# A two-layer sparse graph kernel: one-neighbour tiles without a softmax, two-slot tiles in one group, query products spread over both layers, gathers in small pieces

## The chip, the cores and the metric

The kernel runs on one core of one Trainium2 chip. The metric is the time of one execution on the device in microseconds (us), the median over repeated runs. A profile is one further execution, recorded by the hardware profiler. The engines are TensorE (PE, with its weight load PEld), VectorE (DVE), ScalarE (ACT) and GpSimd (POOL); each works through its instructions in order. SP only issues DMAs.

## What is computed

Two graph layers over N = 2048 nodes of width 512. The adjacency matrix is sparse (each entry is 1 with a chance of 1/1024, some two neighbours a node).

```python
h = relu(layernorm(x))
# layer 0: attention with 16 heads of 32, W_seq, a1, a2
seq = (h @ W_seq).reshape(N, 16, 32)
scores = leaky_relu(s1[i] + s2[j], 0.2) + (1 - adj) * -65500.0
x = x + elu(softmax(scores) @ seq @ W_out + b_out)
h = relu(layernorm(x))
# layer 1: one head
z = scale * (h @ W_q.T + b_q) @ (h @ W_k.T + b_k).T
z = where(z * adj == 0, -10000.0, z * adj)
x = x + relu(softmax(z) @ (h @ W_v.T + b_v))
```

In layer 0 a node without neighbours attends to all nodes with nearly equal penalties; these are the "lone" rows. In layer 1 a node's query and all keys are folded into one product: u = h @ (W_q.T W_k) + bias, and z is u's dot product with a neighbour's h.

## The kernel before, in words

The nodes are ranked by their number of neighbours and handled in 16 tiles of 128 nodes. `ORDER` gives the order of the tiles, `SLOTS` how many neighbour slots the tile at place t has: 1, 1, 1, 1, 0, 8, 2, 5, 2, 4, 2, 3, 2, 3, 2, 3 for t = 0 to 15. Below, "tile t" is the place in this order. Tiles 0 and 1 hold nodes with exactly one neighbour; tiles 2, 3 and 4 have lone rows too.

Up to about 230 us the program normalises x, multiplies by W_seq, finds the neighbours in adj, ranks the nodes and sums the lone rows' attention head by head. `evacuate(15)` on VectorE ends that part; four matmuls (semaphore `tot_mm`) give the totals that `lone_rows(k)` needs.

**Layer 0** is a loop over k = 0 to 15 (to 17 on VectorE), written out on every engine:

- GpSimd gathers a tile's neighbour rows from DRAM, one indirect DMA a slot (`gather`, semaphore `got[t]`). In its loop over t it computes 1/sqrt(var) with a POW (line 1132), stores x1 (line 1133), gathers as `GATHER[t]` says (line 1121), gathers a late tile of x (line 1138) and stores h1 (line 1141).
- VectorE computes attention weights: `scores(g)` (lines 765 to 769), Exp on ScalarE (line 981), `normalise(g)` (777 to 779). `GROUPS` are tiles that share one softmax: tiles 0 to 3 together, each later one alone. `aggregate(t)` multiplies the rows by the weights (line 793) and adds them (794, 797). In step k VectorE does residual(k - 1) (lines 811 to 818), accumulate(k - 2) (833), norm_bias(k - 1) (825), which waits for the POW, lone_rows(k) for k < 3, normalise for tile k + 2, scores for tile k + 4, aggregate(k + 2).
- TensorE does transposes(k), which waits for aggregate(k), the query product of `U_AT[k]`, transposes_h1(k - 2) and project(k) (line 1214). A query product is u of one tile (`queries`, lines 1233 and 1236). The first waits for `lone_done`, since its PSUM banks hold the totals.
- ScalarE copies between them (lines 997, 1004), forms h1 (1018), the two parts of ELU (1026, 1028), and copies u out (`copy_u`, 989 and 990).

After the loop TensorE does the last query products; between them a matmul with ones sums h over all nodes (line 1260, `h_sum_mm`), which VectorE copies. Two query products follow that sum, and VectorE waits for all sixteen copies before its first layer-1 work (line 941).

**Layer 1**: GpSimd gathers h1 rows (`gather1`, line 1146) and adds each output tile to DRAM (`put`, 1151). VectorE does dot products (893), a softmax for the tiles of each of five `PARTS` and `aggregate1` (930). ScalarE does the Exp of a part (1046, 1047), the rest of the attention sum (`base_of`, 1039), the copies of the transposed tiles (1067) and the outputs (1054). TensorE does `transposes1` (1274) and `products` (1287) with W_v, over six PSUM banks.

## Time and profile before

| | |
|---|---|
| median of 3 runs | 508.01 us (506.52 to 508.14) |
| profiled execution | 511.07 us, span 509.3 us |
| PE busy | 392.0 us (77%) |
| DVE busy | 387.9 us (76%) |
| POOL busy | 277.4 us (54%) |
| ACT busy | 245.2 us (48%) |
| chain of waits | DVE 30%, PE 18%, POOL 12% |

The span is what the engines' records cover; the profiled execution's time holds 1.8 us more. Busy shares are means over stages with different limits, so the rows below are read by stage: layer 0 from about 228 to 386 us, layer 1 from there to 494, then the end. In a row of an engine's time line, the bracket is the idle time before the instruction and what released it; "issue" there means that nothing the profile shows was waited for; a wait for a semaphore whose sender the profile cannot tell is shown so too.

### The profile page before, as it was taken

Reading aid. Unit: us, or ns where it says so; the run is one execution under the profiler, and the core shown is the slowest. Engines: PE = TensorE matmul, PEld = TensorE weight load, DVE = VectorE, ACT = ScalarE, POOL = GpSimd, SP = SyncE. Lnnn points to the kernel's source line nnn. Section 1 sums busy time; section 2 is a strip of 40 time slices with the busy share of each in tenths; the row PEclk is TensorE's granted clock in tenths of the full one; section 3 lists DMA queues with packets and bytes.
Section 4 is the critical chain, followed back from the end, with each engine's and each line's share of the span. In section 5 each row is a group of like instructions: output and inputs, shape, how many; then the busy total and the mean of one; then the engine's idle time right before and its main releaser. Section 6 shows DMA issues by size and latency. Waiting matters only on the chain.

```text
span 509.3 us, 6170 instructions
## 1 busy us (share of the span) xinstructions
PE 392.0 (77%) x2018; PEld 280.7 (55%) x2018; DVE 387.9 (76%) x763; ACT 245.2 (48%) x513; POOL 277.4 (54%) x274
## 2 busy tenths in 40 slices
PE   0199999886368998887649899998998196787950
PEld 0187887664267787785336576655577143343520
DVE  1996699998759999898869899879740579997200
ACT  1424696786189999782223343534441242233310
POOL 1640563124568477785668656853547758862330
PEclk9999999998679999899959899999999589888995
DMA  7955399941000134235444423532225657764450
GB/s 268 413 198 175 147 307 348 352 177 64 6 8 5 19 108 107 85 90 168 129 160 115 138 81 121 175 127 82 81 86 161 204 121 163 174 143 62 57 71 3
DMA packets 24196, 70.04 MB, mean 138 GB/s; under 512 B 6113, under 2 KB 6369, under 8 KB 21985
## 3 DMA queue, kind: packets, MB, share of 16 engines
q0 software_dynamic: 14336, 42.63, 31.0%
q1 hardware_dynamic: 8432, 25.38, 13.9%
q10 hardware_dynamic: 1392, 1.61, 1.0%
q8 instruction: 17, 0.28, 0.2%
q14 instruction: 19, 0.15, 0.1%
HBM read 52.48 MB, written 17.12 MB: 137 GB/s over the span
## 4 chain that ended last, share of the span: by engine, by line
DVE 30%; PE 18%; POOL 12%; issue 8%; ACT 2%; DMA 1%; another core or an unknown queue 0%; DVEq 0%; ACTq 0%
PE psum L1287 4%; PE psum L1196 4%; POOL s_shared L1121 4%; PE psum L1236 3%; DVE w_seq L893 3%; DVE s_shared L723 3%; PE psum L1214 3%; DVE s_shared L716 2%; DVE s_shared L714 2%; POOL s_rs L1132 2%; DVE h_t L930 2%; DVE s_x L730 2%; POOL s_shared L1104 2%; DVE s_shared L930 1%; POOL record_dram L1088 1%
## 5 line engine op out<-in xcount | busy, mean ns | idle before, releaser
L969 ACT ACTIVATE s_shared<-psum,seq_all 128x320 bf16<-128x320 f32 x192 | 81.7, 584 | 6.7 <-PE psum L1196 5.6
L1196 PE MATMUL psum<-s_shared 128*128 128x198 bf16 x768 | 74.2, 256 | 2.3 <-POOL s_shared L1104 2.3
L1196 PEld LDWEIGHTS psum<-s_shared 128*128 128x128 bf16 x768 | 69.8, 99 | 7.5 <-POOL s_shared L1104 3.9
L506 PE MATMUL psum<-w_seq,hT 128*128 128x272 f32 x256 | 61.6, 394 | 1.0 <-ACT u_bias_bc L356 1.0
L1236 PE MATMUL psum<-w_qk,s_early 128*128 128x257 f32 (+1 forms) x256 | 60.7, 391 | 0.0
L1214 PE MATMUL psum<-w_out,hT 128*128 128x512 f32 x128 | 59.2, 607 | 0.0
L506 PEld LDWEIGHTS psum<-w_seq,hT 128*128 128x128 f32 x256 | 47.4, 190 | 10.4 <-issue 1.3
L1236 PEld LDWEIGHTS psum<-w_qk,s_early 128*128 128x128 f32 x256 | 49.1, 197 | 7.3
L1104 POOL TENSOR_TENSOR s_shared<-s_shared 128x1056 f32<-128x1056 f32 x16 | 31.2, 1950 | 21.1 <-DVE s_shared L716 21.1
L1121 POOL DMA_INDIRECT s_shared<-seq_dram,tab x28 | 36.1, 1290 | 10.9 <-issue 8.2
L1018 ACT ACTIVATE h_t<-s_x,s_nm,s_rs 128x512 f32<-128x512 f32 x16 | 13.0, 815 | 54.8 <-DVE s_nm L825 54.8
L1214 PEld LDWEIGHTS psum<-w_out,hT 128*128 128x128 f32 x128 | 25.0, 195 | 24.6 <-issue 24.1
L451 DVE FIND_INDEX8 tab<-near,adj_ring 128x8 uint32<-128x2048 f32 x16 | 36.6, 2285 | 0.0
L448 DVE MAX8 near<-adj_ring 128x8 f32<-128x2048 f32 x16 | 36.5, 2283 | 0.0
L226 POOL TENSOR_TENSOR rstd<-veps,power 128x1 f32<-128x1 f32 x16 | 9.0, 562 | 45.2 <-DVE veps L424 45.0
L1151 POOL DMA_INDIRECT out_dram<-s_lone,tab x12 | 20.2, 1679 | 24.7 <-ACT s_lone L1054 23.5
L1132 POOL TENSOR_TENSOR s_rs<-s_ve,power 128x1 f32<-128x1 f32 x16 | 13.8, 862 | 35.3 <-DVE s_ve L818 35.2
L723 DVE TENSOR_SCALAR s_shared<-psum,neg_s 128x320 bf16<-128x320 f32 x64 | 30.7, 541 | 1.2 <-PE psum L1172 1.2
L1287 PE MATMUL psum<-wv_t,bout_bc 128*128 128x512 f32 x64 | 30.8, 627 | 0.0
L1287 PE MATMUL psum<-wv_t,hT 128*128 128x512 f32 x64 | 30.8, 626 | 0.0
L337 ACT ACTIVATE squares<-adj_ring 128x2048 bf16<-128x2048 f32 x16 | 30.4, 1902 | 0.0
L497 PE MATMUL psum<-ident,h_t 128*128 128x128 f32 x64 | 10.9, 298 | 22.8 <-ACT h_t L330 22.8
(242 smaller groups left out, 792.5 us busy)
## 6 DMA issues: line engine op xcount, KB each, us to landing
adj_ring<-in_adj_dram SPq DMA_DIRECT2D x16, 1024.0 KB, 7.5
seq_dram<-seq_all POOLq DMA_DIRECT2D x16, 264.0 KB, 3.5
x_ring<-in_x_dram SPq DMA_DIRECT2D x16, 256.0 KB, 8.0
w_seq<-in_L_gnn_W_seq_dram ACTq DMA_DIRECT2D x1, 1024.0 KB, 7.7
w_q<-in_L_gnn_W_q_dram SPq DMA_DIRECT2D x1, 1024.0 KB, 18.4
w_k<-in_L_gnn_W_k_dram SPq DMA_DIRECT2D x1, 1024.0 KB, 20.4
w_v<-in_L_gnn_W_v_dram SPq DMA_DIRECT2D x1, 1024.0 KB, 6.6
w_out<-in_L_gnn_W_out_dram SPq DMA_DIRECT2D x1, 1024.0 KB, 10.0
```

The source lines that it names most:

```text
L337: act.activation(squares[:, :], adj_ring[:, t % AR, :], ACT.Square, accum_out=square[:, t:t + 1]).then_inc(adj_squared, 1)
L448: step(dve.max(near[:, t, :], adj_ring[:, b, :]))
L451: dve.max_index(record[:, t, 0:TOP], near[:, t, :], adj_ring[:, b, :]).then_inc(adj_searched, 1)
L506: last = pe.matmul(bank[2 + 2 * (t % 2) + i][:, 0:SX // 2], hT[:, t % 2, c * P:(c + 1) * P], w_seq[:, c, i * (SX // 2):(i + 1) * (SX // 2) ...
L723: last = dve.tensor_scalar(ind[i][:, j, PAD:], bank[6 + i][:, 0:LN], neg_s2[:, j - SIGNS, n:n + 1], 2.0, ALU.is_gt, ALU.mult)
L969: last = act.activation(ind[i][:, j, PAD:], bank[4 + i][:, 0:LN], ACT.Sign, bias=seq_all[:, j, D + n:D + n + 1])
L1104: pool.tensor_tensor(split[i][:, :, 2, :], split[i][:, :, 1, :], top_half(split[i][:, :, 1, :]), ALU.subtract).then_inc(r2_done, 1)
L1121: pool.indirect_dma_start(G(t)[:, s, :], None, seq_dram[:, :], bass.IndirectOffsetOnAxis(tab[:, t, s:s + 1], 0)).then_inc(got[t], 16)
L1196: last = pe.matmul(acc(i)[:, k, 0:3 * W2], ind[i][:, j, k * P:(k + 1) * P], rhs.rearrange("p t w -> p (t w)"), start=(j == 0 and k != 1), ...
L1214: last = pe.matmul(bank[2 + k % 2], hidT[:, c * P:(c + 1) * P], w_out[:, c, :], start=False, stop=(c == C - 1))
L1236: last = pe.matmul(bank[4 + 2 * (t % 2) + i][:, 0:hi - lo], h1T(t)[:, c * P:(c + 1) * P], w_qk[:, c, lo:hi], start=False, stop=(c == C - 1))
L1287: last = pe.matmul(bank[2 + t % 6], aT[t % 2][:, c * P:(c + 1) * P], wv_t[:, c, :], start=False, stop=(c == C - 1))
```

## The change

- Tiles 0 and 1 have no scores, weights or aggregate: TensorE transposes their gathered row. Tiles 2 and 3 take the row times `has`, without weights.
- Tile 5's softmax comes first, alone; the five 2-slot tiles 6, 8, 10, 12, 14 share one; the others are alone. `SCORES_AT` puts `scores` in steps 3, 4, 6, 8, 10, 12, and `normalise` one step later. On ScalarE the Exp of scores moves behind ELU.
- residual waits for the first part of ELU for its first half, for the second part for its second.
- Gathered rows lie at fixed places (`LATE`). Nine gathers come first (tiles 6, 8, 7), then two or three in a step.
- Tile 4 has no query product. `U_AT` has one in steps 3 to 6, 8, 10, 12 and 14, four follow before the sum of h, one behind it; 14 and 15 come within layer 1, for k = 4 and 6 (`U1_AT`). The layer-1 products go over four PSUM banks.
- VectorE's constants are computed for tiles 0 to 11 at first, for the others in the last part.

VectorE in step 3 before, from norm_bias(2) (s_nm) to the first addition for tile 5; s_sc are the scores, s_top their maxima and sums, s_early and s_shared the gathered rows.

```order
L825 SCALAR_TENSOR_TENSOR s_nm<-s_mv,s_rs 128x1
L777 TENSOR_REDUCE s_top<-s_sc 128x16
L778 RECIPROCAL s_top<-s_top 128x16
L779 TENSOR_TENSOR s_sc<-s_sc,s_top 128x128
L765 TENSOR_TENSOR s_sc<-s_shared,tab 128x80
L766 SCALAR_TENSOR_TENSOR s_sc<-s_sc 128x80
L767 TENSOR_TENSOR s_sc<-s_sc,s_pen 128x80
L768 TENSOR_REDUCE s_top<-s_sc 128x16
L769 TENSOR_TENSOR s_sc<-s_sc,s_top 128x80
L793 TENSOR_TENSOR s_early<-s_early,s_sc 128x8x512
L794 TENSOR_TENSOR w_seq<-s_early 128x512
```

And now.

```order
L834 SCALAR_TENSOR_TENSOR s_nm<-s_mv,s_rs 128x1
L786 TENSOR_REDUCE s_top<-s_sc 128x16
L787 RECIPROCAL s_top<-s_top 128x16
L788 TENSOR_TENSOR s_sc<-s_sc,s_top 128x128
L775 TENSOR_TENSOR s_sc<-s_shared,tab 128x32 x5
L777 SCALAR_TENSOR_TENSOR s_sc<-s_sc 128x160
L779 TENSOR_TENSOR s_sc<-s_sc,s_pen 128x160
L780 TENSOR_REDUCE s_top<-s_sc 128x80
L781 TENSOR_TENSOR s_sc<-s_sc,s_top 128x160
L805 TENSOR_TENSOR s_early<-s_early,s_sc 128x8x512
L806 TENSOR_TENSOR w_seq<-s_early 128x512
```

Before, a normalisation is followed by the scores of tile 7 (128x80). Now five additions, one a 2-slot tile, and four operations of 160 elements stand between it and the multiplication for tile 5.

GpSimd from the first gathers of layer 0 on, before: L1121 are gathers (s_shared), L1132 the POW, L1133 the store of x1, L1138 a gather of x, L1141 the store of h1.

```order
L1121 DMA s_shared<-seq_dram,tab 128x528 x7
L1132 TENSOR_TENSOR s_rs<-s_ve,power 128x1
L1133 DMA out_dram<-s_x,tab 2048x512
L1121 DMA s_shared<-seq_dram,tab 128x528 x6
L1141 DMA h_dram<-h_t,tab 2048x512
L1132 TENSOR_TENSOR s_rs<-s_ve,power 128x1
L1133 DMA out_dram<-s_x,tab 2048x512
L1121 DMA s_shared<-seq_dram,tab 128x528 x2
```

And now, up to the third POW and what follows it.

```order
L1132 DMA s_shared<-seq_dram,tab 128x528 x9
L1143 TENSOR_TENSOR s_rs<-s_ve,power 128x1
L1144 DMA out_dram<-s_x,tab 2048x512
L1132 DMA s_shared<-seq_dram,tab 128x528 x2
L1152 DMA h_dram<-h_t,tab 2048x512
L1143 TENSOR_TENSOR s_rs<-s_ve,power 128x1
L1144 DMA out_dram<-s_x,tab 2048x512
L1132 DMA s_shared<-seq_dram,tab 128x528 x2
L1152 DMA h_dram<-h_t,tab 2048x512
L1143 TENSOR_TENSOR s_rs<-s_ve,power 128x1
L1144 DMA out_dram<-s_x,tab 2048x512
L1132 DMA s_shared<-seq_dram,tab 128x528 x2
```

Seven first gathers have become nine, six behind the first POW two; the last two shown, behind the third POW, are tile 14's.

TensorE in layer 1 before, from transposes1(4): L1274 are transposes1, L1285 and L1287 products.

```order
L1274 MATMUL psum<-ident,h_t 128x128 x4
L1285 MATMUL psum<-bias_rows,ones_b 128x512
L1287 MATMUL psum<-wv_t,bout_bc 128x512 x4
L1285 MATMUL psum<-bias_rows,ones_b 128x512
L1287 MATMUL psum<-wv_t,hT 128x512 x4
L1274 MATMUL psum<-ident,h_t 128x128 x4
L1274 MATMUL psum<-ident,s_shared 128x128 x4
```

And now, where L1248 and L1251 are a query product.

```order
L1291 MATMUL psum<-ident,h_t 128x128 x4
L1302 MATMUL psum<-bias_rows,ones_b 128x512
L1304 MATMUL psum<-wv_t,bout_bc 128x512 x4
L1248 MATMUL psum<-bias_rows,ones_b 128x257
L1251 MATMUL psum<-w_qk,s_early 128x257
...
L1302 MATMUL psum<-bias_rows,ones_b 128x512
L1304 MATMUL psum<-wv_t,hT 128x512 x4
L1291 MATMUL psum<-ident,h_t 128x128 x4
L1291 MATMUL psum<-ident,s_shared 128x128 x4
```

Product 14 stands between products(3) and products(4), ahead of transposes1(5). Product 15 stands in the same way behind products(5).

The diff, cut to its core:

```diff
-NSLOT = FIRST_SLOT[T]
+NSLOT = FIRST_SLOT[T] - 4
-GROUPS = [(0, 4)] + [(t, 1) for t in range(FULL, T)]
-GATHER = {0: (8, 9), 1: (10,), 2: (11,), 3: (12,), 6: (13,), 7: (14,), 8: (15,)}
-U_AT = {**{k: (k - 3,) for k in range(3, 12)}, 13: (9,), 15: (10,)}
+GROUPS = [(5,), (6, 8, 10, 12, 14), (7,), (9,), (11,), (13,), (15,)]
+SCORES_AT = {3: 1, 4: 2, 6: 3, 8: 4, 10: 5, 12: 6}
+PLACE = {t: p for p, t in enumerate(t for g in GROUPS for t in g)}
+SCORE = {t: sum(SLOTS[i] for i in PLACE if PLACE[i] < PLACE[t]) for t in PLACE}
+LATE = {6: 0, 8: 2, 10: 4, 12: 6, 14: 8, 7: 10, 9: 15, 11: 10, 13: 15, 15: 0}
+FREED_BY = {11: 7, 13: 9, 15: 8}
+GATHER = {0: ((10, 0, 2),), 1: ((12, 0, 2),), 2: ((14, 0, 2),), 3: ((9, 0, 2),), 4: ((9, 2, 4),), 6: ((11, 0, 3),), 8: ((13, 0, 3),), 10: ((15, 0, 3),)}
+NO_SLOT = 4
+U_SEQ = [t for t in range(T) if t != NO_SLOT]
+U_NO = {t: i for i, t in enumerate(U_SEQ)}
+U1_AT = {4: 14, 6: 15}
+U_AT = {3: 0, 4: 1, 5: 2, 6: 3, 8: 5, 10: 6, 12: 7, 14: 8}
...
+            return late[:, LATE[t]:LATE[t] + n, :]
...
+                def group(g):
+                    tiles = GROUPS[g]
+                    K, n, o, p = SLOTS[tiles[0]], len(tiles), SCORE[tiles[0]], PLACE[tiles[0]]
+                    seg = sc[:, o:o + n * K, :].rearrange("p (n k) h -> p n k h", k=K)
+                    best = top[:, p:p + n, :]
+                    return tiles, K, n, seg, best, best.unsqueeze(2).to_broadcast([P, n, K, H])
...
                 def scores(g):
-                    for t in range(t0, t0 + n):
+                    tiles, K, n, seg, best, best_k = group(g)
+                    for i, t in enumerate(tiles):
                         dve.wait_ge(got[t], 16 * K)
-                    step(dve.tensor_tensor(seg, lo[:, :, D:SG].rearrange("p (n k) h -> p n k h", k=K), s1, ALU.add))
+                        last = dve.tensor_tensor(seg[:, i, :, :], G(t)[:, :, D:SG], s1_rank[:, t:t + 1, :].to_broadcast([P, K, H]), ALU.add)
+                        step(last)
                     step(dve.scalar_tensor_tensor(seg, seg, ALPHA, seg, ALU.mult, ALU.max))
...
                 def aggregate(t):
+                    if K == 1:
+                        dve.wait_ge(got[t], 16)
+                        step(dve.tensor_scalar(hb, G(t)[:, 0, 0:D], has[:, t:t + 1], None, ALU.mult))
+                        dve.scalar_tensor_tensor(hb, lone[:, t - LONE0, :], has_not[:, t:t + 1], hb, ALU.mult, ALU.add).then_inc(hid_ready, 1)
+                        return
...
                 def residual(t):
                     b = t % 2
-                    dve.wait_ge(elu_exp, t + 1)
+                    dve.wait_ge(elu_in, t + 1)
...
                     step(dve.scalar_tensor_tensor(x1[:, t, :], bank[2 + b], 0.0, x1[:, t, :], ALU.max, ALU.add))
+                    dve.wait_ge(elu_exp, t + 1)
                     dve.scalar_tensor_tensor(x1[:, t, :], e[b], -1.0, x1[:, t, :], ALU.add, ALU.add).then_inc(x1_ready, 1)
...
                 scores(0)
-                normalise(0)
-                aggregate(0)
                 evacuate(H - 1)
-                aggregate(1)
-                scores(1)
                 dve.wait_ge(tot_mm, 1)
                 dve.wait_ge(fac_exp, 1)
                 lone_rows(0)
                 aggregate(2)
-                starts = {t0: g for g, (t0, n) in enumerate(GROUPS)}
                 for k in range(1, T + 2):
...
-                    if k + 2 in starts:
-                        normalise(starts[k + 2])
-                    if k + 4 in starts and k + 4 > FULL:
-                        scores(starts[k + 4])
+                    if k == 3:
+                        normalise(0)
+                    if k - 1 in SCORES_AT:
+                        normalise(SCORES_AT[k - 1])
+                    if k in SCORES_AT:
+                        scores(SCORES_AT[k])
                     if k + 2 < T:
                         aggregate(k + 2)
...
+                    if t0 == EARLY:
+                        constants(EARLY, T)
...
-                dve.wait_ge(u_copied, T)
+                constants(0, EARLY)
...
-                    if k + 4 in starts and k + 4 > FULL:
-                        exp_scores(starts[k + 4])
...
                         act.activation(e[k % 2], e[k % 2], ACT.Exp, scale=-1.0).then_inc(elu_exp, 1)
-                copy_u(T - 4)
-                copy_u(T - 3)
+                    if k in SCORES_AT:
+                        exp_scores(SCORES_AT[k])
+                copy_u(9)
+                copy_u(10)
+                copy_u(11)
                 copy_h1T(T - 1)
-                copy_u(T - 2)
-                copy_u(T - 1)
+                copy_u(12)
+                copy_u(13)
...
+                    if k in U1_AT:
+                        copy_u(U1_AT[k])
...
-                def gather(t):
-                    if freed_by(t):
-                        pool.wait_ge(hid_ready, freed_by(t))
-                    for s in range(SLOTS[t]):
+                def gather(t, lo, hi):
+                    if t in FREED_BY:
+                        pool.wait_ge(hid_ready, FREED_BY[t] - 1)
+                    for s in range(lo, hi):
...
 
                 pool.wait_ge(mm_done, H)
-                gather(FULL + 1)
-                gather(FULL + 2)
+                for t in (6, 8, 7):
+                    gather(t, 0, SLOTS[t])
...
-                    for k in GATHER.get(t, ()):
-                        gather(k)
-                    if 1 <= t <= T // 2:
+                    for part in GATHER.get(t, ()):
+                        gather(*part)
+                    if 2 <= t < 2 + T // 2:
                         pool.wait_ge(lone_done, LONE)
-                        pool.indirect_dma_start(x1[:, T // 2 + t - 1, :], None, x[:, :],
-                                                bass.IndirectOffsetOnAxis(own[:, T // 2 + t - 1, :], 0)).then_inc(x_late[t - 1], 16)
...
                 def transposes(k):
-                    pe.wait_ge(hid_ready, k + 1)
+                    if k < 2:
+                        pe.wait_ge(got[k], 16)
+                    else:
+                        pe.wait_ge(hid_ready, k - 1)
                     if k:
                         pe.wait_ge(hidT_done, k)
+                    rows = early[:, k, 0:D] if k < 2 else hid[k % 4]
...
                 def queries(t):
-                    pe.wait_ge(h1T_done, t + 1)
-                    if t >= 2:
-                        pe.wait_ge(u_copied, t - 1)
-                    else:
-                        pe.wait_ge(lone_done, LONE)
+                    pe.wait_ge(h1T_done, h1_no(t))
+                    pe.wait_ge(lone_done, LONE)
+                    used = [U_NO[i] for i in U_SEQ if i < t and u_bank(i) == u_bank(t)]
+                    if used:
+                        pe.wait_ge(u_copied, used[-1] + 1)
...
+                pe.wait_ge(evac_done, H - 1)
                 for k in range(T):
                     transposes(k)
-                    for t in U_AT.get(k, ()):
-                        queries(t)
-                    if k >= 2:
+                    if k == 0:
+                        pe.wait_ge(evac_done, H)
...
+                        last.then_inc(tot_mm, 1)
+                    if k in U_AT:
+                        queries(U_AT[k])
+                    if k >= 2 and k - 2 != NO_SLOT:
                         transposes_h1(k - 2)
                     project(k)
-                queries(T - 5)
                 transposes_h1(T - 2)
-                queries(T - 4)
-                queries(T - 3)
+                queries(9)
+                queries(10)
+                queries(11)
                 transposes_h1(T - 1)
+                queries(12)
                 pe.wait_ge(summed, T)
                 pe.wait_ge(hidT_done, T)
                 pe.matmul(bank[0], ones[:, 0:P], h_acc).then_inc(h_sum_mm, 1)
-                queries(T - 2)
-                queries(T - 1)
+                queries(13)
...
                 def products(t):
                     pe.wait_ge(aT_done, t + 1)
-                    if t >= 6:
-                        pe.wait_ge(o_ready, t - 5)
+                    if t >= 4:
+                        pe.wait_ge(o_ready, t - 3)
...
                         transposes1(k)
                         products(k - 1)
+                    if k in U1_AT:
+                        queries(U1_AT[k])
```

## Rows read from the trace of the kernel before

**Rows 1.** Stages: us and length, engines' busy time (instructions), clock, DMA share, GB/s.

```profile
280.00:362.00 82.00, 74.96 (x309) 49.72 (x308) 72.22 (x167) 35.89 (x74) 51.41 (x46) 0.98 0.35 116
```

**Rows 2.** VectorE in time: start, us, line, operation, [idle before <-releaser].

```profile
232.30 0.68 DVE L791 TENSOR_TENSOR w_seq<-s_early,s_sc 128x512 f32<-128x512 f32 x1
...
256.52 0.16 DVE L825 SCALAR_TENSOR_TENSOR s_nm<-s_mv,s_rs 128x1 f32<-128x1 f32 x1 [2.77 <-POOL s_rs L1132]
...
263.64 0.69 DVE L811 SCALAR_TENSOR_TENSOR s_x<-psum,s_x 128x512 f32<-128x512 f32 x1 [1.10 <-ACT bout_bc L1028]
...
282.79 0.18 DVE L777 TENSOR_REDUCE s_top<-s_sc 128x16 f32<-128x32 f32 x1
...
283.51 0.19 DVE L765 TENSOR_TENSOR s_sc<-s_shared,tab 128x32 f32<-128x32 f32 x1
...
284.52 1.22 DVE L793 TENSOR_TENSOR s_shared<-s_shared,s_sc 128x1024 f32<-128x1024 f32 x1
...
354.49 0.68 DVE L811 SCALAR_TENSOR_TENSOR s_x<-psum,s_x 128x512 f32<-128x512 f32 x1
...
362.09 0.68 DVE L811 SCALAR_TENSOR_TENSOR s_x<-psum,s_x 128x512 f32<-128x512 f32 x1
...
395.06 0.28 DVE L941 TENSOR_SCALAR hT<-seq_all 128x16 f32<-128x16 f32 x1 [8.40 <-issue]
```

**Rows 3.** TensorE in time, columns as in rows 2.

```profile
261.18 0.59 PE L1233 MATMUL psum<-bias_rows,ones_b 128*128 128x257 bf16 x2 [9.51 <-DVE s_lone L847]
...
261.56 6.18 PE L1236 MATMUL psum<-w_qk,s_early 128*128 128x257 f32 x16
...
372.88 0.38 PE L1233 MATMUL psum<-bias_rows,ones_b 128*128 128x257 bf16 x2
...
376.57 0.60 PE L1223 MATMUL psum<-ident,h_t 128*128 128x128 f32 x4
...
384.84 1.02 PE L1260 MATMUL psum<-s_shared,ones 128*128 128x512 f32 x2
...
433.88 1.07 PE L1274 MATMUL psum<-ident,s_shared 128*128 128x128 f32 x4 [4.94 <-DVE s_shared L930]
...
439.92 3.60 PE L1287 MATMUL psum<-wv_t,hT 128*128 128x512 f32 x8
...
443.36 0.60 PE L1274 MATMUL psum<-ident,s_shared 128*128 128x128 f32 x4
...
447.83 1.11 PE L1274 MATMUL psum<-ident,h_t 128*128 128x128 f32 x4 [3.88 <-DVE h_t L930]
```

**Rows 4.** The chain of waits: start, us, what.

```profile
455.18 4.20 DMA w_out<-h_dram,tab
```

**Rows 5.** GpSimd in time, columns as in rows 2.

```profile
231.84 0.94 POOL L1121 DMA_INDIRECT s_shared<-seq_dram,tab  x1 [2.61 <-PE psum L1196]
...
239.63 1.15 POOL L1121 DMA_INDIRECT s_shared<-seq_dram,tab  x1 [0.30 <-issue]
...
270.07 4.85 POOL L1121 DMA_INDIRECT s_shared<-seq_dram,tab  x1 [0.30 <-issue]
...
325.26 0.81 POOL L1132 TENSOR_TENSOR s_rs<-s_ve,power 128x1 f32<-128x1 f32 x1
...
326.26 1.05 POOL L1133 DMA_INDIRECT out_dram<-s_x,tab  x1 [0.19 <-issue]
...
327.62 0.98 POOL L1121 DMA_INDIRECT s_shared<-seq_dram,tab  x1 [0.31 <-issue]
...
335.22 0.59 POOL L1132 TENSOR_TENSOR s_rs<-s_ve,power 128x1 f32<-128x1 f32 x1
```

**Rows 6.** The eight gathers of x rows in the loop (line 1138).

```profile
DMA to landing us min/median/max: 3.3/3.7/3.9
```

**Rows 7.** ScalarE in time, columns as in rows 2.

```profile
367.77 0.58 ACT L1004 ACTIVATE hT<-psum 128x512 f32<-128x512 f32 x1
...
446.36 0.22 ACT L1046 ACTIVATE hT<-hT 128x24 f32<-128x24 f32 x1 [1.77 <-DVE hT L910]
```

124 lines of the change are left out of this document (53 added, 71 removed).

## Prediction

> **What bounds the kernel now.** I read the page's stages first, then the two busiest engines in order of time from 228 us on (the diff changes nothing of what runs before that), then the chain of waits. k is a step of the first layer's loop; R(t) is the start of residual(t) on VectorE, which opens step k = t + 1.
>
> From 280 to 362 us VectorE and TensorE are both nearly full: 72.2 and 75.0 us busy in 82 [rows 1]. VectorE hardly ever waits there; a step is its own work plus the short wait for the POW on GpSimd. R(2), R(12) and R(13) stand at 263.64, 354.49 and 362.09 [rows 2]. Two places before are different: norm_bias(1) waits 2.77 us, because GpSimd issues six gathers between two POWs, and residual(2) waits 1.10 us for ScalarE [rows 2]. TensorE stands 9.51 us for lone_done before its first query product [rows 3]. After R(13) TensorE's order decides: the column sum of h ends at about 385.9 [rows 3]. Then VectorE stands 8.40 us, until query tiles 14 and 15 are copied, and begins its first dot product's preparation at 395.06 [rows 2]. In the second layer VectorE, GpSimd (the last gather of h lands 4.20 us after its issue [rows 4]) and, over the last 27 us, TensorE follow each other.
>
> **The change part by part**, as shifts of times against the profiled execution (minus is earlier).
>
> *Up to R(2).* Tiles 0 and 1 lose their softmax and their product, but VectorE then only waits longer for the totals from TensorE, since evacuate(15), which ends where the product of 232.30 starts, comes no sooner: nothing. Tile 2 loses a product of 0.7 as that one [rows 2], but seven first gathers become nine. They begin at 231.84 and the seventh ends at 240.78 [rows 5], 1.28 each, so the ninth ends near 243.4 and POW(0) after it: norm_bias(0) gains 0.3 only. Tile 3 loses its product: 0.7. With two gathers instead of six behind POW(0), the wait of 2.77 falls to about 0.7: 2.0. Tile 6's own scores leave: 1.0, the length 283.51 to 284.52 of another 2-slot tile [rows 2]. ScalarE's Exp of scores now stands behind the ELU and no longer holds it: 1.1. Sum -5.1. Waiting for elu_in alone before the first half of residual adds nothing where VectorE is late anyway.
>
> *Steps 3 to 13.* Five 2-slot softmaxes become one. Left out: five normalisations of 0.72 (282.79 to 283.51) and four more scorings of 1.01 [rows 2], -7.6. Added: five first additions of 0.22 and four wide operations of about 0.4, 2.7; one wide normalisation, 1.5. The wide ones, of 160 elements, are estimates from the 0.2 that an operation of 32 takes, five of them in 1.01 [rows 2]. The scores of tiles 7, 9, 11, 13 and 15 only move.
>
> Then a **new wait**. scores(1), of all five tiles, stands in step 3 directly behind normalise(0) and ahead of aggregate(5), and it needs tile 14's two rows. Their gathers are issued in the same step, behind POW(2) and the store of x1. From the end of a POW: 0.19 and 1.05 for the store, 0.30, 0.98 for a gather, 0.31; the second gather starts 2.8 us after the POW [rows 5]. Landing takes 3.3 to 3.9 us in the eight gathers of x rows [rows 6], so 6.5 after the POW. VectorE is there after about 2.0 (normalise(0) and four additions, an estimate from rows 2). It stands 4.5 us, with aggregate(5) and all later steps behind it. Bounds: 0, if the landing were hidden, and 6, with the 4.20 us landing [rows 4] and a held-up issue.
>
> GpSimd is the other new limit. A step in which it issues three gathers, an x row and two stores lasts 9.96 us from POW to POW (325.26 to 335.22) [rows 5]. Before, VectorE's step beside it was about 8.7. Now the gathers of tiles 11, 13 and 15 lie beside steps of 8.9, 7.6 and 7.6 (354.49 to 362.09 is one with three slots and no scores [rows 2]). The third has no x row: 8.7. Waits: 0.8, 2.2 and 1.0, together 4.0, of which 1.1 stood in the old sum. Bounds 0 and 6.
>
> Sum of steps 3 to 13: -7.6 + 2.7 + 1.5 + 4.5 + 4.0 - 1.1 = +4.0. So R(13) shifts by -1.1 only.
>
> A gather is lengthened while VectorE multiplies: the one at 270.07 took 4.85 us beside the multiplication of 4096 elements that began at 269.67, against 0.98 of another [rows 5]. That is in the 9.96. The Trainium skill ("SBUF — State Buffer", Who interferes with whom) infers that a tensor_tensor does not hinder the writing of descriptors, though it contends with a GpSimd operation that reads SBUF. By the first, the three-gather step would be some 1.1 us shorter and the sum 2.5 us lower, near 500.4. The 4.85 us row speaks for the second, as a gather reads its indices; I stay with the row.
>
> *The end of layer 0.* Steps 14 and 15. Before, h's column sum ended 23.8 after R(13). Now project(15) waits for the copy of hidden(15), which ends 6.3 after R(13) (368.35 before [rows 7]) and which a query product used to cover. Then in TensorE's order: project(15) 3.65 (eight matmuls of this size last 3.60), transposes 0.44, three products of 3.69, transposes 0.44, one more 3.69, the sum's matmuls 1.06 [rows 3]: 26.7 after R(13), +2.9. Removing queries from the steps before helps little, since four stand ahead of the sum as before. TensorE has just stood 2 to 3 us. After longer waits its work took longer: a query product 6.18 after 9.51 idle, against 3.69, and 9.5 from 433.88 to 443.36 after 4.94 idle, for transposes and two products that take 7.7 at full clock [rows 3]. I add half of the smaller loss, 0.8; bounds 0 and 4.2, both losses.
>
> *Between the layers.* constants(0, 12) needs only copies that were made long before. The 8.40 us go: -8.4, with product 13 beside VectorE's dots. The gathers of h then lead the first dot by 8 instead of 12 us. Dot 3's row is issued fourth and lands about 7.5 us after the first issue: in time.
>
> *Layer 1.* Product 14 (3.69) falls before TensorE's 4.94 us wait, and is hidden. Product 15 falls before the 3.88 us wait [rows 3]; but ScalarE's Exp at 446.36 [rows 7] stands behind the transposes that it delays. These move from 443.36 to 445.4 only, since with the shorter wait ahead the 1.8 us lost to the clock come back, and their copy is done near 446.6. I count 0.3. Four PSUM banks instead of six for the outputs cost nothing: each output was read more than a product earlier. The second constants call adds two small operations, 0.45. Sum +0.75; bounds 0 and 7.8.
>
> Total: -5.1 + 4.0 + 3.7 - 8.4 + 0.75 = -5.1. The profiled execution took 511.07 us (span 509.3, 1.8 around it) and becomes 506.0. The median of the runs shown is 3.1 below it, and I take the shift from there: 508.0 - 5.1 = 502.9.
>
> **Rivals.** *The gathers are in time.* The waits for tile 14 and behind three gathers do not come: -4.5 and -4.0, 494.4. For it: GpSimd is often idle before a POW in the old trace. Against: the four intervals worked out above all come from its rows.
>
> *Layer 1 pays for the products.* TensorE runs in order, and the transposes behind each product feed ScalarE, whose Exp feeds VectorE, whose weights release the output, the store ahead of the last gathers, and so the last dots. If the waits at 433.88 and 447.83 cover nothing, two products come in full, 7.4 instead of 0.3: 510.0, slower. It turns the sign once 5.4 of the 7.4 stay on the path (the 5.1 gained and the 0.3 counted already). Against: both covers stand in the rows, 8.8 us in all.
>
> *Every late gather waits twice.* Tiles 11, 13 and 15 are gathered two steps ahead of their aggregation, no longer three. If each row lands 1.7 us after VectorE asks for it, on top of the POW, 5.1 come back: 508.0, and the change does not do what it says, splitting work without shortening the path.
>
> **How the numbers follow.** Forecast 0.52 (499.5 to 506), gathers in time 0.18, layer 1 pays 0.16, late gathers wait twice 0.14. Below 495.5 lies over half of the second case, above 509 over half of the third: 2 in 10 are outside. What a measurement of this kernel can tell from no change is about 0.3%, 1.5 us. Faster: 0.51 + 0.18 + 0.03 = 0.72. Same: 0.01 + 0.02 + 0.07 = 0.10. Slower: 0.14 + 0.04 = 0.18.
>
> **What would show it.** VectorE standing 4 to 5 us within step 3, released by a gather and followed by the 4.4 us multiplication. R(13) within 2 us of 362. POWs about 10 us apart where three gathers stand, with norm_bias waiting 1 to 2.7. The sum's matmuls 25 to 29 us after R(13). No wait over 1 us between the copy of that sum and the first dot. Query products 14 and 15 where TensorE stood idle. I am wrong if R(13) comes before 358, or if the second layer lasts over 3 us longer from its first preparation to the end.

## The result and the profile after

| | before | changed |
|---|---|---|
| median of 8 runs | 507.69 us (505.93 to 508.43) | 503.97 us (502.04 to 505.86) |
| ratio | | 0.993, 95% interval 0.9905 to 0.9955 |
| profiled execution, span | 511.07, 509.3 us | 502.33, 500.7 us |
| DVE, PE, POOL busy | 387.9, 392.0, 277.4 us | 379.3, 390.5, 275.3 us |
| chain of waits | DVE 30%, PE 18%, POOL 12% | DVE 27%, POOL 22%, PE 10% |

The time fell by 3.7 us; 5.1 was forecast. The two spans differ by 8.6 us, more than the medians, so the kernel before was profiled a second time (below).

VectorE's time line of the changed kernel: start, length, engine, line, operation, and in brackets the wait before it.

```profile
251.93 0.16 DVE L834 SCALAR_TENSOR_TENSOR s_nm<-s_mv,s_rs 128x1 f32<-128x1 f32 x1 [0.47 <-POOL s_rs L1143]
...
268.01 0.19 DVE L775 TENSOR_TENSOR s_sc<-s_shared,tab 128x32 f32<-128x32 f32 x1 [5.60 <-DMA s_shared<-seq_dram,tab]
...
269.56 4.42 DVE L805 TENSOR_TENSOR s_early<-s_early,s_sc 128x4096 f32<-128x4096 f32 x1
...
308.85 2.29 DVE L805 TENSOR_TENSOR s_shared<-s_shared,s_sc 128x2048 f32<-128x2048 f32 x1
...
317.91 0.16 DVE L834 SCALAR_TENSOR_TENSOR s_nm<-s_mv,s_rs 128x1 f32<-128x1 f32 x1 [1.51 <-POOL s_rs L1143]
...
325.41 1.76 DVE L805 TENSOR_TENSOR s_shared<-s_shared,s_sc 128x1536 f32<-128x1536 f32 x1
...
334.45 0.16 DVE L834 SCALAR_TENSOR_TENSOR s_nm<-s_mv,s_rs 128x1 f32<-128x1 f32 x1 [2.75 <-POOL s_rs L1143]
...
349.74 0.16 DVE L834 SCALAR_TENSOR_TENSOR s_nm<-s_mv,s_rs 128x1 f32<-128x1 f32 x1 [1.50 <-POOL s_rs L1143]
350.43 0.21 DVE L775 TENSOR_TENSOR s_sc<-s_shared,tab 128x48 f32<-128x48 f32 x1 [0.53 <-DMA s_shared<-seq_dram,tab]
...
360.98 0.68 DVE L819 SCALAR_TENSOR_TENSOR s_x<-psum,s_x 128x512 f32<-128x512 f32 x1
...
387.74 0.69 DVE L952 COPY w_seq<-psum 128x512 f32<-128x512 f32 x1 [10.43 <-PE psum L1278]
388.35 0.16 DVE L904 TENSOR_SCALAR hT<-seq_all 128x12 f32<-128x12 f32 x1
...
450.80 0.69 DVE L899 CUSTOM_DVE_ANT_0 w_seq<-seq_all,w_out 128x512 f32<-128x512 f32 x1 [1.63 <-DMA w_out<-h_dram,tab]
```

The reader is to see: the wait of 2.77 for the POW before norm_bias(1) [rows 2] is 0.47; a new wait of 5.60 us stands where the forecast put 4.5, released by a gather and followed by the 4.42 us multiplication for tile 5; three longer waits for the POW stand behind the steps with three gathers; R(13) is at 360.98, 1.1 earlier than in [rows 2], though 0.9 of this lies ahead of E (below), where both kernels do the same; and the 8.40 us between the copy of the column sum and the first preparation of layer 1 are gone (387.74, then 388.35).

GpSimd's time line of the same execution:

```profile
241.20 0.95 POOL L1132 DMA_INDIRECT s_shared<-seq_dram,tab  x1 [0.30 <-issue]
242.17 0.60 POOL L1143 TENSOR_TENSOR s_rs<-s_ve,power 128x1 f32<-128x1 f32 x1
...
309.43 2.56 POOL L1132 DMA_INDIRECT s_shared<-seq_dram,tab  x1 [0.31 <-issue]
...
323.57 0.96 POOL L1143 TENSOR_TENSOR s_rs<-s_ve,power 128x1 f32<-128x1 f32 x1 [1.13 <-DVE s_ve L827]
...
326.06 1.96 POOL L1132 DMA_INDIRECT s_shared<-seq_dram,tab  x1 [0.31 <-issue]
...
333.84 0.58 POOL L1143 TENSOR_TENSOR s_rs<-s_ve,power 128x1 f32<-128x1 f32 x1
...
380.52 0.97 POOL L1157 DMA_INDIRECT s_shared<-h_dram,tab  x1 [2.51 <-DMA h_dram<-h_t,tab]
...
407.05 1.64 POOL L1162 DMA_INDIRECT out_dram<-s_lone,tab  x1 [0.30 <-issue]
...
446.58 0.95 POOL L1157 DMA_INDIRECT w_out<-h_dram,tab  x1 [0.30 <-issue]
```

POW(8) to POW(9) takes 10.27 us with three gathers, where [rows 5] showed 9.96. And from the first gather of h at 380.52 to the last at 446.58 GpSimd has no gap but its usual 0.3. Its share of the chain of waits is 22%, against 12% in the first trace of before and 18% in the second: the chain now runs through these gathers and puts. TensorE's late products stand where it would have waited:

```profile
415.89 3.63 PE L1251 MATMUL psum<-w_qk,s_early 128*128 128x257 f32 x16
...
424.27 0.66 PE L1291 MATMUL psum<-ident,s_shared 128*128 128x128 f32 x4 [0.66 <-DVE s_shared L943]
...
428.64 3.63 PE L1251 MATMUL psum<-w_qk,s_early 128*128 128x257 f32 x16
...
438.62 0.66 PE L1291 MATMUL psum<-ident,h_t 128*128 128x128 f32 x4 [2.26 <-DVE h_t L943]
```

The waits of 4.94 and 3.88 [rows 3] are 0.66 and 2.26, and both products take the 3.63 us of full clock. The transposes and the two products behind the first wait took 9.5 us before and take 7.8 now, 4.15 ahead of product 15 and 3.65 behind it:

```profile
424.98 3.60 PE L1304 MATMUL psum<-wv_t,bout_bc 128*128 128x512 f32 x8
...
439.40 5.22 PE L1304 MATMUL psum<-wv_t,bout_bc 128*128 128x512 f32 x8
```

Behind the 2.26 us that are left of the second wait, eight matmuls still take 5.22 us (second row) and not 3.60.

### The profile page after: what moved, and what is told of

The parts are those of the page before. It is cut to its first block, busy times and chain, and to the rows that moved or that the text cites. A ratio compares the mean times of both kernels' runs of the same rounds, so it can differ in the third digit from the quotient of the medians.

```text
span 500.7 us, 6093 instructions
## 1 busy us (share of the span) xinstructions
PE 390.5 (78%) x1996; PEld 276.8 (55%) x1996; DVE 379.3 (76%) x725; ACT 242.9 (49%) x505; POOL 275.3 (55%) x274
## 4 chain that ended last, share of the span: by engine, by line
DVE 27%; POOL 22%; PE 10%; issue 8%; DMA 3%; ACT 2%; DVEq 0%; ACTq 0%; POOLq 0%
POOL s_shared L1132 4%; PE psum L1304 4%; POOL s_shared L1157 4%; POOL s_x L1157 3%; DVE s_shared L730 3%; PE psum L1207 3%; DVE s_shared L723 3%; DVE s_shared L721 3%; POOL out_dram L1162 3%; POOL s_rs L1143 2%; DVE s_shared L805 2%; DMA s_shared<-seq_dram,tab 2%; POOL s_shared L1115 2%; DVE s_st L823 2%; DVE s_x L821 2%
## 5 line engine op out<-in xcount | busy, mean ns | idle before, releaser
L1229 PE MATMUL psum<-w_out,hT 128*128 128x512 f32 x128 | 61.4, 625 | 0.0
L1251 PE MATMUL psum<-w_qk,s_early 128*128 128x257 f32 x240 | 57.8, 395 | 0.0
L515 PEld LDWEIGHTS psum<-w_seq,hT 128*128 128x128 f32 x256 | 47.4, 190 | 10.4 <-issue 1.3
L1251 PEld LDWEIGHTS psum<-w_qk,s_early 128*128 128x128 f32 x240 | 46.8, 200 | 7.1
L1132 POOL DMA_INDIRECT s_shared<-seq_dram,tab x28 | 34.8, 1243 | 10.9 <-issue 8.2
```

What stands on the lines that cost most here:

```text
L515: last = pe.matmul(bank[2 + 2 * (t % 2) + i][:, 0:SX // 2], hT[:, t % 2, c * P:(c + 1) * P], w_seq[:, c, i * (SX // 2):(i + 1) * (SX // 2) ...
L1132: pool.indirect_dma_start(G(t)[:, s, :], None, seq_dram[:, :], bass.IndirectOffsetOnAxis(tab[:, t, s:s + 1], 0)).then_inc(got[t], 16)
L1229: last = pe.matmul(bank[2 + k % 2], hidT[:, c * P:(c + 1) * P], w_out[:, c, :], start=False, stop=(c == C - 1))
L1251: last = pe.matmul(bank[u_bank(t) + i][:, 0:hi - lo], h1T(t)[:, c * P:(c + 1) * P], w_qk[:, c, lo:hi], start=False, stop=(c == C - 1))
```

## The experiments

The twelve runs were made in three sets, the first on one chip, the others on another; the result above was taken apart from them. All times below are counted from E, the start of evacuate(15)'s last reduction (line 730 before, 737 after), since everything ahead of it is the same work and shifts by up to 2.2 us between executions:

```profile
231.60 0.78 DVE L730 TENSOR_REDUCE s_x<-psum 128x198 f32<-128x594 f32 x1 [0.95 <-PE psum L1196]
...
230.68 0.78 DVE L737 TENSOR_REDUCE s_x<-psum 128x198 f32<-128x594 f32 x1 [2.67 <-PE psum L1207]
```

The first row is of the kernel before, the second of the changed kernel. S is the first preparation of layer 1 on VectorE. "g first" and "g last" are the starts of the first and last gather of h on GpSimd. Each number is the difference of two starts in the run's time lines, or of the span and E.

```
kernel              set  R(2)   R(13)   h sum copied  g first  g last  end     ratio to before
before (rows)        -   32.04  130.49  154.37        151.48   223.58  277.70
changed, first       -   26.14  130.30  157.06        149.84   215.90  270.02  0.993
a0 changed           1   26.13  129.54  156.30        149.79   228.21  282.68  1.001  (0.9982 to 1.0038)
e1 early gathers     1   26.10  124.72  152.16        144.94   223.52  277.52  0.9876 (0.9834 to 0.9919)
e2 spread gathers    1   26.15  127.02  153.78        146.55   226.37  280.72  0.9944 (0.9917 to 0.997)
e4 no group          1   26.15  125.25  152.01        144.79   224.42  279.56  0.9918 (0.9891 to 0.9945)
x1 before            2   32.03  130.60  156.08        153.18   221.34  275.50
x3 late copy         2   26.13  130.01  156.77        149.55   215.78  270.37  0.9941 (0.9919 to 0.9963)
e3 split products    2   26.14  128.36  155.70        148.48   214.68  269.58  0.9914 (0.9885 to 0.9943)
e5 products back     2   26.14  129.73  156.49        149.26   226.67  280.86  1.0136 (1.0116 to 1.0156)
a1 changed           3   26.13  130.18  156.93        149.70   215.71  270.00  0.9956 (0.9935 to 0.9976)
e7 product 9 back    3   26.14  129.69  154.55        151.01   218.24  273.23  0.998  (0.9964 to 0.9996)
e9 put later         3   26.13  129.97  156.73        149.50   213.88  269.63  0.9899 (0.9864 to 0.9934)
e8 all               3   26.10  120.19  146.95        139.71   205.62  259.57  0.9755 (0.9722 to 0.9788)
```

Medians of the kernel before in the three sets: 515.53, 506.83 and 506.57 us.

**Both kernels again.**

> The kernel before once more, for a second trace. In the second trace of the changed kernel TensorE's completion of query product 13 reached ScalarE 8.9 us after its modelled end, and the transposes behind it 5 us after theirs, while GpSimd issued its 21 gathers of h without a gap: those 14 us are the whole loss against the first trace (512.6 against 500.7 us). If such a stall belongs to the gathers' burst, the kernel before has it too where its last products end inside the burst: S (the first preparation of layer 1) or the first Exp of layer 1 would come up to 14 us later than the 395.06 and 399.73 of its first trace, on a machine where its time is near 515; where its time is near 508 it would have none, or the 1 to 3 us of the first trace. If the stall belongs to the changed code alone, the time of the kernel before near 515 must come from somewhere else in its trace.

> The changed kernel a third time, as the measure for the others of this set. Expected 0.993 of the kernel before where ScalarE does not stand in front of layer 1's first Exp, and 1.001 where it does, as it did in the second trace (8.7 us of VectorE there).

> The changed kernel once more, beside the variants of this set, so that they can be compared with it and not only with the kernel before. Expected: its ratio to the kernel before again near 0.993, its norm_bias waits and its 5.6 us wait for tile 14's row in step 3 as in the first trace. If the two profiled executions differ by 2 us or more in span, then the 8.6 us between the two first traces hold that much of chance.

x1: 507.09 us, span 505.3. No stall stands in it. Its first gather of h on GpSimd:

```profile
382.98 0.97 POOL L1146 DMA_INDIRECT s_shared<-h_dram,tab  x1 [2.50 <-DMA h_dram<-h_t,tab]
```

and R(13) and S on VectorE:

```profile
360.40 0.69 DVE L811 SCALAR_TENSOR_TENSOR s_x<-psum,s_x 128x512 f32<-128x512 f32 x1
...
393.89 0.17 DVE L941 TENSOR_SCALAR hT<-seq_all 128x16 f32<-128x16 f32 x1 [7.33 <-ACT seq_all L990]
```

From E to the end it is 2.2 us shorter than the first trace of before: 0.6 longer up to S, 2.8 shorter from there (111.41 us to the end of the span, against 114.24). Against this trace the changed kernel is 5.5 us shorter.

a1: 504.40 us, the times from E within 0.2 us of the first trace. Its medians here and in the result lie 2.2 and 3.7 below the kernel before, its traces 5.5 below x1: both profiled executions of the changed kernel are among its fastest (its runs lie between 501.65 and 506.03 in set 3), and what makes the others slower wasn't seen.

a0 is the surprise: on the first set's chip both kernels were near 515, and no gain can be told there (1.001). Up to the first gather of h it is the changed kernel to 0.8 us. Then this stands on VectorE:

```profile
399.88 0.16 DVE L930 TENSOR_TENSOR hT<-hT,s_others 128x4 f32<-128x4 f32 x1 [8.66 <-issue]
```

on ScalarE:

```profile
398.89 0.39 ACT L998 ACTIVATE seq_all<-psum 128x257 f32<-128x257 f32 x1 [12.93 <-remote]
...
408.72 0.60 ACT L1076 ACTIVATE hT<-psum 128x512 f32<-128x512 f32 x1 [6.50 <-remote]
```

and on TensorE:

```profile
386.32 3.63 PE L1251 MATMUL psum<-w_qk,s_early 128*128 128x257 f32 x16
402.62 1.94 PE L1291 MATMUL psum<-ident,h_t 128*128 128x128 f32 x8 [12.66 <-DVE h_t L943]
```

ScalarE's copy of product 13 begins 8.9 us after the modelled end of that product (389.95), the copy of the first transposes 4.2 us after the eight of them end (404.56). Both wait for TensorE ("remote" names no sender). In e1, e2 and e4 the same copy comes 14.6, 15.4 and 12.5 us after the product's end (VectorE's waits there are 14.24, 15.04 and 12.23), in no trace of sets 2 and 3. The late copy of product 13 lies inside GpSimd's 21 gathers of h without a gap (379.71 to 405.78 in a0); the second late copy comes 2.9 us after them, and sets 2 and 3 have the same 21 gathers and no late copy, so the gathers alone don't make it. Why it happens on one chip and not on the other is open, and whether the kernel before has it there too: it was not profiled on it. So the missing gain of set 1 isn't explained either. And since these waits differ between the traces of set 1, R(13), which lies ahead of them, tells more than its medians.

**The order of two gathers (e1).**

```
-GATHER = {0: ((10, 0, 2),), 1: ((12, 0, 2),), 2: ((14, 0, 2),), ...
+GATHER = {0: ((14, 0, 2),), 1: ((7, 0, 3),), 2: ((7, 3, 5),), ...
-                for t in (6, 8, 7):
+                for t in (6, 8, 10, 12):
```

> The gathers of tile 14 move from behind POW(2) to behind POW(0); tile 7's five go behind POW(1) and POW(2) instead, and those of tiles 10 and 12 ahead of the first POW. Theory A (the wait in step 3 is on the path, and nothing takes it back later): VectorE no longer stands 5.6 us before tile 14's scores, R(3) to R(13) and the first gather of h all come 5 to 6 us earlier, the time falls by 5.6 to about 498.4. Theory B (TensorE, whose project(4) ends only 4 us before the end of that wait, and GpSimd take over): R(3) comes 5 us earlier but R(13) less than 3, and the time falls by under 3 us.

R(13) came 4.8 us earlier than in a0 and 5.6 earlier than in the changed kernel's first trace; the median is 6.1 below a0's. The wait for tile 14 is gone:

```profile
262.79 1.10 DVE L775 TENSOR_TENSOR s_sc<-s_shared,tab 128x32 f32<-128x32 f32 x5
263.92 0.32 DVE L777 SCALAR_TENSOR_TENSOR s_sc<-s_sc 128x160 f32<-128x160 f32 x1
...
265.24 4.42 DVE L805 TENSOR_TENSOR s_early<-s_early,s_sc 128x4096 f32<-128x4096 f32 x1
```

Theory A, which forecast 5 to 6 us. TensorE had room.

**No group (e4).**

```
-GROUPS = [(5,), (6, 8, 10, 12, 14), (7,), (9,), (11,), (13,), (15,)]
-SCORES_AT = {3: 1, 4: 2, 6: 3, 8: 4, 10: 5, 12: 6}
+GROUPS = [(t,) for t in range(FULL, T)]
+SCORES_AT = {k: k - 2 for k in range(3, 13)}
```

> The two-slot tiles have softmaxes of their own again, one step ahead of their aggregation; everything else is as in the changed kernel, the places of the gathers too. By the terms of the prediction the group saves 7.6 - 2.7 - 1.5 = 3.4 us of VectorE's work and costs the wait for tile 14, which measured 5.6: theory A expects R(13) 2.2 us earlier without the group and the time 2.2 lower, near 501.8. Theory B (small operations are cheaper in the shadow of the waits for the POW than counted, or the wait would have stood for another gather anyway): no difference or slower.

The direction held, the size didn't: R(13) 4.3 us earlier than in a0, the median 5.2 lower. From R(2) to R(13) the waits fall from 14.8 to 5.9 us: tile 14's 4.98 go, and of the three behind three gathers only one is left, 1.51 us, since the work that comes back stands beside the gathers. The work itself, what is left of the stretch without the waits, grows from 88.6 to 93.3 us: 4.7 and not 3.4, mostly because tile 6's scores (1.0) come back in these steps too, which the expectation had left out. Net of both, 4.3. With tile 14's gathers where the change puts them, the group costs more than it saves; with e1's order it is ahead of e4 by 0.5 us at R(13).

**Gathers spread, and multiplications split (e2, e3).**

```
-... 6: ((11, 0, 3),), 8: ((13, 0, 3),), 10: ((15, 0, 3),)}
+... 5: ((11, 0, 1),), 6: ((11, 1, 3),), 7: ((13, 0, 1),), 8: ((13, 1, 3),), 9: ((15, 0, 1),), 10: ((15, 1, 3),)}
```

> The three gathers each of tiles 11, 13 and 15 no longer stand in one step: one goes into the step before, two stay. Theory A (GpSimd's issues bound these steps): the waits of norm_bias at the three places, 1.51, 2.75 and 1.50 us, and the 0.53 for tile 15's row fall from 4.9 us over the usual 0.46 to about 2.2 in all (most of it behind POW(8)), R(13) comes 2.7 us earlier and the time falls by 2.7 to about 501.3. Theory B (the waits only move into the short steps, which have no room for one more gather): R(13) and the time within 1 us of the changed kernel.

R(13) 2.5 us earlier than a0, the median 3.3 lower; one wait of 1.52 is left, behind POW(8), and 0.63 for tile 15's row. Theory A: GpSimd's issues bounded these steps.

```
-                    step(dve.tensor_tensor(rows, rows, w, ALU.mult))
+                    if t in (9, 11, 13):
+                        for s in range(K):
+                            last = dve.tensor_tensor(rows[:, s:s + 1], rows[:, s:s + 1], w[:, s:s + 1], ALU.mult)
+                        step(last)
+                    else:
+                        step(dve.tensor_tensor(rows, rows, w, ALU.mult))
```

> The multiplications of tiles 9, 11 and 13 by their weights (2048, 1536, 1536 elements) are made as one instruction per slot of 512. They run beside the first gather of the three steps with three gathers. Theory A (GpSimd's writing of a gather's descriptors is held until VectorE's running multiplication ends; in the trace such a gather ends 0.85 us after the multiplication in four cases out of four): those gathers fall from 2.56, 1.96 and 1.96 us to under 1.6, the waits of norm_bias behind them by 0.7 to 1 each, VectorE pays 0.1 to 0.3 per tile for the extra instructions, and the time falls by 1 to 1.5. Theory B (a tensor_tensor does not hinder descriptor writing; the gather is long for another reason): the gathers stay at 2 to 2.6 us and the time rises by about 0.5.

GpSimd's time line of e3:

```profile
308.75 0.97 POOL L1137 DMA_INDIRECT s_shared<-seq_dram,tab  x1 [0.30 <-issue]
310.02 1.48 POOL L1137 DMA_INDIRECT s_shared<-seq_dram,tab  x1 [0.30 <-issue]
...
324.54 1.49 POOL L1137 DMA_INDIRECT s_shared<-seq_dram,tab  x1 [0.31 <-issue]
```

and VectorE's beside it:

```profile
308.17 2.50 DVE L807 TENSOR_TENSOR s_shared<-s_shared,s_sc 128x512 f32<-128x512 f32 x4
```

The same work in four instructions takes VectorE 2.50 instead of 2.29 us, and the gather beside it 0.97 instead of 2.56, the next 1.48 instead of 1.13; R(13) came 1.65 to 1.95 us earlier than in x3 and the first trace. Theory A for the gathers. The wait for the POW behind the first of the three steps is back at its usual 0.46, the next fell from 2.75 to 1.50, and the last is back at the usual too; but 1.56 us stand before tile 15's scores instead of 0.62 (x3). In the median 501.68 against x3's 503.34 of the same set; the intervals overlap, and the end of the trace came only 0.8 us earlier than in x3, so the gain in the time is not shown.

**The products before layer 1 again (e5), and the late copy of product 13 (x3).**

```
-U1_AT = {4: 14, 6: 15}
+U1_AT = {}
...
-                    if t0 == EARLY:
-                        constants(EARLY, T)
...
-                constants(0, EARLY)
+                constants(0, T)
...
                 copy_u(13)
+                copy_u(14)
+                copy_u(15)
...
                 queries(13)
+                queries(14)
+                queries(15)
```

> Query products 14 and 15 stand behind product 13 again, ahead of layer 1, and one constants call over all 16 tiles waits for the copies of all. The rest is the changed kernel. The prediction says that this wait was worth 8.4 us and layer 1's two products 0.3: theory A expects VectorE to stand about 8.5 us after its copy of the column sum, and the time 7 to 8 us over the changed kernel. Theory B (GpSimd's gathers of h, issued without a gap from about 380 us, bound layer 1, so that VectorE has room there): the wait comes back as VectorE's, but the time rises by 3 to 6 only.

513.35 us, 9.4 above the changed kernel's first median and 10.0 above x3, which is the changed kernel but for one copy and ran in the same set. VectorE's first work of layer 1:

```profile
400.88 0.17 DVE L904 TENSOR_SCALAR hT<-seq_all 128x16 f32<-128x16 f32 x1 [13.16 <-ACT seq_all L997]
```

The wait is 13.16 and not 8.5, for three products and not two follow the sum, and they share one pair of PSUM banks, so that 14 and 15 each wait 0.84 for the copy before. From E, S is 12.7 us later than in the first trace, the end 10.8: about 1.9 of the delay was hidden. Neither theory's size; theory B's reason holds for 1.9 us only. For the rest the late start of VectorE reaches GpSimd, whose first put stands still for ScalarE's output:

```profile
416.21 1.83 POOL L1162 DMA_INDIRECT out_dram<-s_lone,tab  x1 [10.13 <-ACT s_lone L1063]
```

```
-                copy_u(13)
...
+                    if k == 1:
+                        copy_u(13)
```

> The copy of query product 13 no longer stands on ScalarE ahead of layer 1's first Exp; it is made after the second copy of transposed rows. Everything else is the changed kernel. Where the stall shows (9 to 15 us before the first Exp): theory A (only the signal of product 13, the last work ahead of a wait of TensorE, is late) expects the Exp at its usual 0.7 us after VectorE's weights and the time 9 or more us lower; theory B (TensorE itself stands still) expects the first transposes of layer 1 to end late instead, and a gain under 3 us. Where no stall shows: within 0.5 us of the changed kernel, 0.993 of the kernel before.

There was no stall in its set: 0.9941, as expected. It says nothing on the stall, and so whether only the signal of product 13 is late or TensorE itself stands was not tested.

**What sets the start and the length of layer 1 (e7, e9).**

```
-U_AT = {3: 0, 4: 1, 5: 2, 6: 3, 8: 5, 10: 6, 12: 7, 14: 8}
+U_AT = {3: 0, 4: 1, 5: 2, 6: 3, 8: 5, 10: 6, 12: 7, 14: 8, 15: 9}
...
-                copy_u(9)
...
-                queries(9)
```

> Query product 9 stands in step 15 ahead of project(15), where it covers the copy of hidden(15), as in the kernel before, and no longer behind it. The prediction counted 2.9 us for that missing cover. Theory A (the column sum of h sets the start of layer 1): the sum's matmuls end 1.8 us earlier and the time falls by that. Theory B (GpSimd's gathers of h set it, which begin 8.7 us after R(15)): R(15), and the first gather with it, come 1.7 us later, and the time rises by 1 to 1.7.

VectorE's time line of e7 at R(15) and at the copy of the sum:

```profile
374.17 0.69 DVE L819 SCALAR_TENSOR_TENSOR s_x<-psum,s_x 128x512 f32<-128x512 f32 x1 [3.67 <-ACT u_bias_bc L1032]
...
386.42 0.69 DVE L952 COPY w_seq<-psum 128x512 f32<-128x512 f32 x1 [6.74 <-PE psum L1276]
```

The last gather of h:

```profile
450.11 0.95 POOL L1156 DMA_INDIRECT w_out<-h_dram,tab  x1 [0.30 <-issue]
```

The copy of the sum came 2.4 us earlier than in a1, the first gather of h 1.3 later, the last 2.5 later, and the median rose from 504.40 to 505.76 (the intervals of the ratios overlap; in the traces the end came 3.2 later). Theory B: from the changed kernel on, an earlier sum gains nothing, and later gathers of h cost. Only 1.3 of the last gather's 2.5 us come from the start; the other 1.2 are longer issues (the 39 gathers took 41.5 us instead of 40.0), for a reason no trace shows.

```
-                for t in range(9):
+                for t in range(10):
                     gather1(t)
                 for t in range(T):
                     put(t)
-                    if 9 + t < T:
-                        gather1(9 + t)
+                    if 10 + t < T:
+                        gather1(10 + t)
```

> GpSimd issues tile 9's four gathers of h ahead of the first put, so that each put stands one tile's gathers later and one put less stands before the last gather. Theory A (GpSimd, busy without a gap from the first gather of h to the last, bounds layer 1 up to there): the last gather lands 1.9 us earlier, VectorE's wait of 1.63 for it goes, the time falls by about 1.6. Theory B (VectorE bounds it and that wait is its own slack, or ScalarE's outputs wait for buffers that the late puts free): no gain, or up to 3 us slower.

The last gather came 1.8 us earlier (g last), the median 1.9 lower than a1's, the wait for its row 0.95 instead of 1.32. In the one trace the end came 0.4 earlier only. Theory A's size by the medians; but the wait did not go, as it expected, and the trace leaves open how 1.8 us at the last gather would reach the end.

**All together (e8)**: the edits of e1, e2, e3 and x3.

> Three edits that helped alone, in one kernel, and the late copy of product 13: tile 14's gathers behind POW(0) (R(13) 5.6 us earlier alone), one of each three gathers a step earlier (3.3 alone), multiplications of tiles 9, 11 and 13 per slot (1.9 alone). Theory A (each takes away its own wait): R(13) comes 9 to 10 us earlier against evacuate(15), since the second and third edits share what is left behind POW(8), and all of it reaches the end, for GpSimd's gathers of h start as much earlier: about 494.5 where the changed kernel takes 504, 0.975 of the kernel before. Theory B (another engine takes over: TensorE's products in the steps, now 7.3 us apart, need 7.3 to 8.6 us a step): R(13) comes 6 to 7 us earlier only, 0.981.

493.87 us, 10.5 below a1; R(13) 10.0 and the end 10.4 us earlier. Theory A, to the number. No wait for the POW over 0.7 us is left in the loop, and from R(2) to R(13) VectorE waits 5.1 us in all, against 15.5 in a1. Behind the first step that had three gathers, and at R(13), VectorE shows:

```profile
310.83 0.16 DVE L839 SCALAR_TENSOR_TENSOR s_nm<-s_mv,s_rs 128x1 f32<-128x1 f32 x1 [0.46 <-POOL s_rs L1149]
...
350.22 0.68 DVE L824 SCALAR_TENSOR_TENSOR s_x<-psum,s_x 128x512 f32<-128x512 f32 x1
```

## Why the prediction was right, and where it wasn't

The sign, the range and the mechanism of layer 0 held. The closeness of the total is partly luck: against the second trace of before the five terms missed by -0.8, +1.6, -2.4, +1.0 and +0.2 us, which nearly cancel. Term by term, from E, against both traces of before:

- *Up to R(2)*, forecast -5.1: measured -5.9. norm_bias(0) gained 0.7 and not 0.3, for a gather takes 1.25 us and the ninth ended at 242.15, just as the POW was wanted; the wait behind POW(0) fell by 2.3 and not 2.0.
- *Steps 3 to 13*, forecast +4.0: measured +5.7 and +5.6 (R(13) less R(2)). The wait for tile 14 was 5.6 instead of 4.5 and the waits behind three gathers 4.4 over the usual 0.46, and 0.5 for tile 15's row, instead of 4.0. The forecast's own intervals (9.96 less 8.9 and 7.6, 8.7 less 7.6) give 1.1, 2.4 and 1.1, where it wrote 0.8, 2.2 and 1.0; 1.05, 2.29 and 1.04 came. What is left, 3.7 us less work, is the forecast's -7.6 + 2.7 + 1.5 = -3.4. So R(13) hardly moved, as said (-0.2 and -0.3 from E, forecast -1.1); e1 and e2 take the two waits away one by one, and "the gathers are in time" falls. Its price was sound: e8, where nearly all these waits are gone, runs at 493.87, and that case was put at 494.4.
- *R(13) to the sum's copy*, forecast +3.7: measured +2.9 against the first trace, +1.3 against the second. From R(13) to the end of the sum's matmuls it took 26.65 us, as forecast without the clock (26.7); the 0.8 for the clock did not come, for the clock stayed at its upper level (2.4 GHz), as the row below says. Against the second trace the term is smaller because that one itself took 25.4 us, and not the 23.8 of [rows 3].

The busy times of the stretch from 362 to 395 us of the changed kernel (PE, PEld, DVE, ACT, POOL, then the granted clock, DMA share and GB/s):

```profile
362.00:395.00 33.00, 28.06 (x124) 20.37 (x122) 15.35 (x48) 10.98 (x25) 20.12 (x21) 1.00 0.39 128
```

- *Between the layers*, forecast -8.4: -8.5 and -7.4.
- *Layer 1*, forecast +0.75 from S to the end: +0.9 against the second trace (112.35 less 111.41). Against the first it is -1.9, since that one was 2.8 us longer from S on than the second, with more waits of GpSimd (below).

The sum against the second trace is -5.5, forecast -5.1; the medians gave -3.7 and, in set 3, -2.2.

The step that was wrong in its reason is the path between the layers. I followed the column sum and its wait. Two paths meet in layer 1: VectorE's, which starts at S, and that of GpSimd's gathers of h, which starts 8.7 us after R(15) in every trace but a0's (9.4). Before, these began 151.5 and 153.2 after E, now 149.8, and from there GpSimd needs 66 us without a gap to the last one (72 and 68 before). I had seen the sum as late and not seen R(15) as early. Against the first trace, 5.7 of the 6.0 us by which the gathers' stretch is shorter are gaps of GpSimd; against the second there were hardly any gaps to remove (0.41 us before one put, 0.3 being usual), and the same 46 issues took 54.1 us instead of 52.1, for a reason not shown. There the last gather is 5.4 earlier, 3.3 by the start and 2.1 by the shorter stretch, and the end 5.5. e5 and e7 say how the paths stand in the changed kernel: of an S that is 12.7 us later 1.9 are hidden, and a sum 2.4 us earlier gains nothing. So the forecast's -8.4 came as VectorE's, but what it was worth in the time is set by GpSimd, and that the total agrees owes something to luck.

"Layer 1 pays for the products" fell: from S to the end the changed kernel needs 112.35 us, and e5, which has no query product there, 110.52, so the two cost 1.8 us at most and not 7.4. "Every late gather waits twice" fell too: behind three gathers only tile 15's row was waited for, 0.53 us. That a gather is lengthened by a multiplication beside it, where I stayed with the row, is what e3 showed.

## What to carry to other kernels

A change that takes work from the busiest engine gains only what its neighbours' issues don't fill: here a group of softmaxes saved VectorE 3.7 us of work, and its waits in the same steps grew by 9.4. When several tiles share one operation, ask for the last of their inputs first, and gather that one first. Then follow each engine's first and last instruction of a stage: one without gaps is the first candidate for the bound, whatever the longest wait was, and an experiment that moves its start alone, as e7 nearly does, tells.
